# A weight rounding that reads 32-bit tanh values and rounds by adding a constant, instead of a 16-bit integer copy

## The chip, the core and the metric

The kernel runs on one core of one Trainium2 chip. The core has TensorE (matrix products, written to PSUM), VectorE and GpSimd (elementwise work and reductions), ScalarE (activation functions) and SyncE, whose queue issues the DMAs. Each engine works through its own instructions in the order in which they are written; semaphores make one engine wait for another. The metric is device time in microseconds (us), the median of several executions.

## What is computed

For each of 8 batches of 512 rows of width 512, a masked cross-attention over 64 context rows is added to x. Then a gated feed-forward layer with quantized activations and ternary weights (hidden width 2048) is added. The change concerns the ternary weights:

```
def _ternary_quant(w):
    s = jnp.mean(jnp.abs(w))
    wq = jnp.round(jnp.tanh(w / (s + EPS))) * jnp.arctanh(s)
    return w + jax.lax.stop_gradient(wq - w)

def _linear_bit(x, w, g):
    xq = _act_quant(_rmsnorm(x, g))
    wq = _ternary_quant(w)
    return jnp.einsum('bsd,od->bso', xq, wq)

swish = jax.nn.silu(_linear_bit(x, w1, g1))
x_v = _linear_bit(x, w2, g2)
h = swish * x_v
return _linear_bit(h, w3, g3)
```

round(tanh(...)) is -1, 0 or 1; the factor arctanh(s) is applied later, to the result of the product.

## The kernel before

**Tiles.** The 4096 rows are 32 tiles of 128 rows (`NT`), four to a batch (`TPB`). The hidden width is cut into four chunks of 512 (`CH`); the gate works chunk by chunk, `gate(t, 0)` to `gate(t, 3)`.

**Start-up, about the first 95 us.** Each of the three weights comes as 32-bit numbers in four pieces (`WC = 4`, `WN = 2048` elements in each of 128 partitions): the first into `stageA` (the half of `X` that later batches will use), the second into `stageB` (later the space of `hp`, `gh` and `c3`), the third into `stageA` again, piece by piece, once the first weight's piece has been rounded (`load_w3` waits for `s_w1_q`). For each weight: absolute sums of the pieces (`weight_abs`, part on ScalarE, part on VectorE), a matmul with ones that adds over the partitions (`weight_total`), mean and reciprocal on VectorE (`weight_mean`), then for each piece a tanh on ScalarE (`weight_tanh`, L676) and a rounding on VectorE (`weight_round`, L917), which leaves a 16-bit float piece of `W1q`, `W2q` or `W3q`. There are twelve tanh and twelve roundings. Meanwhile GpSimd computes arctanh of the mean as a series of one-column steps, each waiting for the one before (`arctanh_series`, L521 to L527), and from it `wc`; `asc = aa * wc` (L466) is the scale of the silu.

**Between them** stands the first attention and the first tiles: `stage_a_gain` (L826, row times gain, VectorE), `stage_a_root` (avk and ak, L454 and L459, GpSimd), `quantize_12` (L478, GpSimd), a DMA transpose into `q12T`, `up` (L1080, TensorE, which waits for the rounded chunk: `s_w1_q`, `s_w2_q`), `silu` (L655, ScalarE), `gate` (L857, VectorE, silu times second product, into `hp`), `gain_3` (L489, GpSimd, `hp` times the third gain), `max_3` (L863, VectorE), `stage_h_factor`, `quantize_3` (L647, ScalarE), two DMA transposes, `down` (L1092, 16 matmuls, TensorE), `result` (L894, VectorE).

**The loop.** `slot(b, j)` of each engine is one tile's share of that engine's work, in an order written out by hand; it overlaps tile t's up-projection with the down-projection of tile t - 2. The roundings stand at fixed places of VectorE's order: the first weight's 0 at 30 us, 1 at 36, 2 and 3 at 44 directly behind the second's 0; the second's 1 at 48, 2 at 54, 3 at 59; the third's 0 at 82, 1 at 86, 2 and 3 at 88 to 90.

Of the kernel before, what the change touches and what calls it, by code (L numbers as in the profile page):

```python
# [15 lines left out]
ALU = mybir.AluOpType  # L16
ACT = mybir.ActivationFunctionType
# [2 lines left out]
BF16 = mybir.dt.bfloat16  # L20
U8 = mybir.dt.uint8
F16 = mybir.dt.float16
I16 = mybir.dt.int16

P = 128
NEG = 1e30
# [5 lines left out]
MAGIC = 1.5 * 2.0 ** 23  # L32
# [4 lines left out]
def bit_ffn_xattn(nc, x, xT, ctx_rows, mask, maskT, w1T, w2T, w3T, g1, g2, g3, out):  # L37
# [13 lines left out]
    WN = D * H // P // WC  # L51
# [3 lines left out]
    with ExitStack() as ctx:  # L55
        def sb(name, shape, dt=F32):
            return ctx.enter_context(nc.sbuf_tensor(name, shape, dt))
# [53 lines left out]
        winv = sb("winv", [P, 3])  # L111
# [154 lines left out]
        W1f = W1q[:, :, :, :].rearrange("p c k n -> p (c k n)")  # L266
        W2f = W2q[:, :, :, :].rearrange("p c k n -> p (c k n)")
        W3f = W3q[:, :, :].rearrange("p k n -> p (k n)")
# [320 lines left out]
        def _(act):  # L589
# [82 lines left out]
            def weight_tanh(i, src, k, done):  # L672

                act.wait_ge(s_w_inv, i + 1)
                part = slice(k * WN, (k + 1) * WN)
                nc.scalar.activation((W1f, W2f, W3f)[i][:, part].bitcast(I16), src[:, part], ACT.Tanh,  # L676
                                     scale=winv[:, i:i + 1]).then_inc(done, 1)

            def logs(c0, c1, n):
                act.wait_ge(s_coef_arg, 2 * c1)  # L680
# [7 lines left out]
            weight_abs(0, stageA, 2, s_w1_abs)  # L688
            attention_probT(0)
            weight_tanh(0, stageA, 0, s_w1_tanh)  # L690
            weight_tanh(0, stageA, 1, s_w1_tanh)
            stage_a_var(0)
            weight_tanh(0, stageA, 2, s_w1_tanh)
            weight_tanh(0, stageA, 3, s_w1_tanh)
            for k in range(2, WC):
# [61 lines left out]
        def _(dve):  # L757
# [155 lines left out]
            def weight_round(src, dst, k, done_tanh, done):  # L913

                dve.wait_ge(done_tanh, k + 1)
                part = slice(k * WN, (k + 1) * WN)
                nc.vector.tensor_copy(dst[:, part], dst[:, part].bitcast(I16)).then_inc(done, 1)  # L917


            nc.vector.memset(ones[:, :], 1.0).then_inc(s_const_ones, 1)  # L920
# [15 lines left out]
            weight_abs(1, stageB[:, :], 0, s_w2_abs)  # L936
            attention_x1(0, 0)
            weight_round(stageA, W1f, 0, s_w1_tanh, s_w1_q)
            weight_abs(1, stageB[:, :], 1, s_w2_abs)
            dve.wait_ge(s_gains_in, 32)  # L940
            stage_a_gain(0)
            stage_a_max(0)
            stage_a_factor(0, 0)
            weight_round(stageA, W1f, 1, s_w1_tanh, s_w1_q)
            weight_mean(1)
            attention_x1(0, 1)
            attention_cc(1)
            weight_round(stageB[:, :], W2f, 0, s_w2_tanh, s_w2_q)
            weight_round(stageA, W1f, 2, s_w1_tanh, s_w1_q)
            weight_round(stageA, W1f, 3, s_w1_tanh, s_w1_q)  # L950
# [220 lines left out]
```

## Time and profile before

| | us |
|---|---|
| three runs | 476.87, 477.88, 479.64 |
| median | 477.88 |
| the profiled execution | 479.64 |
| its span, first to last instruction | 477.4 |

| engine | busy in the profiled execution |
|---|---|
| TensorE (PE) | 413.4 us, 87% |
| VectorE (DVE) | 400.3 us, 84% |
| ScalarE (ACT) | 351.0 us, 74% |
| GpSimd (POOL) | 331.5 us, 69% |

The profile takes one execution, here the slowest of the three; 2.24 us of it lie outside the span. Engines overlap, so the busy times don't add up to anything; what ends late in each stretch has to be read from the waits. In a row of the timeline the first number is the start in us from the span's start, the second the time from the first start to the last end, then engine, line of the kernel, operation, output and inputs, shapes, and how many instructions are merged in the row; in brackets, how long the engine sat idle before it and what ended that.

### The profile page before, as it was taken

How to read it: one execution, taken by the hardware profiler on the slowest of the kernel's cores; microseconds unless marked ns; L12 is line 12 of the kernel's file. 1: busy time of each engine (PE TensorE's matmuls, PEld its weight loads, DVE VectorE, ACT ScalarE, POOL GpSimd, SP SyncE). 2: the span in 40 equal slices, each digit the busy share in tenths (PEclk: the TensorE clock that was granted, in tenths of full speed). 3: DMA queues.
4: the chain of work that ended last, by engine and by line, in shares of the span. 5: the costliest groups of instructions: out<-in, count | busy, mean ns of one | idle time of the engine just before them, and what ended most of it. 6: DMA issues, size and time to landing. Idle time of an engine off the chain costs nothing. (4 is left out here: it accounts for less than half of the span.)

```text
span 477.4 us, 8317 instructions
## 1 busy us (share of the span) xinstructions
PE 413.4 (87%) x1910; PEld 195.3 (41%) x1910; DVE 400.3 (84%) x913; ACT 351.0 (74%) x608; POOL 331.5 (69%) x535
## 2 busy tenths in 40 slices
PE   0634876899999999999999999999999999899964
PEld 0611622345533464446444644464446434334421
DVE  2496785899999989999999999999999999887550
ACT  1678779987888789867987698869886976565560
POOL 0146647897877777778777877877877878767530
PEclk9999676999999999999999999999999999899988
DMA  6998742354775466645664457455745344435334
GB/s 262 385 384 280 268 176 38 116 110 111 171 174 89 110 181 133 136 110 114 166 170 90 112 144 182 86 119 147 181 86 120 77 88 89 90 78 97 68 70 85
DMA packets 112615, 67.96 MB, mean 142 GB/s; under 512 B 102864, under 2 KB 102992, under 8 KB 108880
## 3 DMA queue, kind: packets, MB, share of 16 engines
q1 hardware_dynamic: 112592, 67.72, 55.1%
q8 instruction: 7, 0.11, 0.1%
q14 instruction: 16, 0.13, 0.1%
HBM read 34.14 MB, written 8.39 MB: 89 GB/s over the span
## 5 line engine op out<-in xcount | busy, mean ns | idle before, releaser
L489 POOL TENSOR_TENSOR stageB<-stageB,g3b 128x512 f32<-128x512 f32 x128 | 164.6, 1290 | 55.0 <-DVE stageB L857 54.2
L1080 PE MATMUL S<-W2q,q12T 128*128 128x512 f16 x512 | 135.7, 389 | 7.4 <-DVE stageB L857 6.1
L1080 PE MATMUL S<-W1q,q12T 128*128 128x512 f16 x512 | 136.0, 389 | 3.8 <-ACT sg L655 2.4
L1092 PE MATMUL DN<-W3q,stageB 128*128 128x512 f16 x512 | 121.3, 391 | 15.4 <-DMA stageB<-stageB 13.7
L655 ACT ACTIVATE sg<-S,asc 128x512 f32<-128x512 f32 x128 | 87.7, 686 | 59.0 <-PE S L1080 53.0
L857 DVE TENSOR_TENSOR stageB<-sg,S 128x512 f32<-128x512 f32 x128 | 86.9, 679 | 16.8 <-ACT sg L655 10.1
L863 DVE TENSOR_REDUCE hm<-stageB 128x1 f32<-128x512 f32 x128 | 86.5, 677 | 1.5 <-POOL stageB L489 1.5
L1092 PEld LDWEIGHTS DN<-W3q,stageB 128*128 128x128 f16 x512 | 49.9, 100 | 81.4 <-issue 26.0
L1080 PEld LDWEIGHTS S<-W2q,q12T 128*128 128x128 f16 x512 | 49.7, 99 | 74.5 <-DVE stageB L857 14.0
L1080 PEld LDWEIGHTS S<-W1q,q12T 128*128 128x128 f16 x512 | 49.6, 100 | 70.6 <-issue 10.0
L662 ACT ACTIVATE junk<-stageB 128x1024 bf16<-128x1024 f32 x64 | 67.3, 1052 | 6.6 <-DVE stageB L857 6.0
L647 ACT ACTIVATE stageB<-stageB,hf 128x1024 f16<-128x1024 f32 x64 | 69.8, 1141 | 2.4 <-DVE hf L880 2.4
L826 DVE SCALAR_TENSOR_TENSOR ga<-X,anm,g12b 128x512 f32<-128x512 f32 x64 | 56.6, 923 | 4.0 <-POOL c L478 2.3
L478 POOL TENSOR_SCALAR c<-ga,af 128x512 f16<-128x512 f32 x64 | 44.0, 699 | 2.1 <-DVE af L848 2.0
L637 ACT ACTIVATE junk_a<-X,anm 128x512 bf16 (+1 forms) x32 | 23.0, 718 | 25.7 <-POOL anm L448 25.7
L832 DVE TENSOR_REDUCE am<-ga 128x2 f32<-128x1024 f32 x32 | 38.8, 1211 | 0.1
L894 DVE SCALAR_TENSOR_TENSOR X<-DN,hsc,X 128x512 f32 (+1 forms) x32 | 24.0, 751 | 16.8 <-PE DN L1092 11.4
L1040 PE MATMUL R<-ccT,xTs 128*128 128x64 f32 x256 | 36.0, 309 | 2.4 <-ACT ccT L594 2.4
L1040 PEld LDWEIGHTS R<-ccT,xTs 128*128 128x128 f32 x256 | 35.9, 225 | 3.9 <-ACT ccT L594 3.1
L459 POOL TENSOR_TENSOR ak<-avk,mhalf 128x1 f32<-128x1 f32 x32 | 27.7, 865 | 2.7
L817 DVE SCALAR_TENSOR_TENSOR X<-R,rval,X 128x512 f32 (+1 forms) x32 | 22.6, 743 | 0.0
L1059 PE MATMUL R<-ctxr,probT 64*128 64x512 f32 x64 | 20.0, 703 | 2.6 <-DVE X L817 2.6
(96 smaller groups left out, 387.4 us busy)
## 6 DMA issues: line engine op xcount, KB each, us to landing
xTs<-in_xT SPq DMA_DIRECT2D x8, 1024.0 KB, 7.1
X<-in_x SPq DMA_DIRECT2D x8, 1024.0 KB, 6.0
out_x<-X SPq DMA_DIRECT2D x32, 256.0 KB, 3.0
X<-in_w1T SPq DMA_DIRECT2D x4, 1024.0 KB, 12.9
stageB<-in_w2T SPq DMA_DIRECT2D x4, 1024.0 KB, 21.5
X<-in_w3T SPq DMA_DIRECT2D x4, 1024.0 KB, 6.5
ctxr<-in_ctx SPq DMA_DIRECT2D x16, 128.0 KB, 3.0
ctxc<-in_ctx SPq DMA_DIRECT2D x8, 128.0 KB, 4.3
```

The source lines that it names most:

```text
L478: nc.gpsimd.tensor_scalar(c12[:, i * D:(i + 1) * D], ga[:, i, :], af[:, i:i + 1], QUANTUM, ALU.mult, ALU.mult).then_inc(s_c12_made, 1)
L489: nc.gpsimd.tensor_tensor(gh[q][:, part], hp[:, part], g3b[:, part], ALU.mult).then_inc(s_gh_made, 1)
L647: nc.scalar.activation(c3[:, part], gh[q][:, part], ACT.Copy, scale=hf[:, :]).then_inc(s_c3_made, 1)
L655: nc.scalar.activation(sg[n % 2][:, :], S1[n % 2][:, :], ACT.Silu, scale=asc[z][:, 0:1])\
L662: nc.scalar.activation(junk[:, h * HALF:(h + 1) * HALF], hp[:, h * HALF:(h + 1) * HALF], ACT.Square, accum_out=hss[:, h:h + 1]).then_inc(s ...
L826: nc.vector.scalar_tensor_tensor(out=ga[:, i, :], in0=xtile(t), scalar=anm[:, :], in1=g12b[:, i, :], op0=ALU.add, op1=ALU.mult).then_inc(s ...
L832: nc.vector.tensor_reduce(am[:, :], ga[:, :, :], AX_X, ALU.max, apply_absolute_value=True)\
L857: nc.vector.tensor_tensor(hp[:, n * CH:(n + 1) * CH], sg[n % 2][:, :], S2[n % 2][:, :], ALU.mult)\
L863: nc.vector.tensor_reduce(hm[:, n:n + 1], gh[q][:, n * CH:(n + 1) * CH], AX_X, ALU.max, apply_absolute_value=True).then_inc(s_gh_max, 1)
L1040: mm = nc.tensor.matmul(R[1][:, j * M:(j + 1) * M], xTs[:, k, j, :], ccT[:, k, :], start=(k == 0), stop=(k == KD - 1))
L1080: mm = nc.tensor.matmul(bank[n % 2][:, :], q12T[q][:, i * KD + k, :], w[:, n, k, :], start=(k == 0), stop=(k == KD - 1))
L1092: mm = nc.tensor.matmul(DN[:, :], q3T[:, k, :], W3q[:, k, :], start=(k == 0), stop=(k == KH - 1))
```

## The change

Before, the tanh writes its values as 16-bit integers into the space of the 16-bit float weight (the conversion rounds them), and VectorE copies them in place from integer to float: 16 bits in, 16 bits out. After, the tanh writes 32-bit floats in place over the loaded piece, and VectorE reads these, adds and subtracts `MAGIC` = 1.5 x 2^23 in one instruction (which rounds to whole numbers) and writes the 16-bit float weight: 32 bits in, 16 bits out. Semaphores, waits and the order of the instructions on every engine stay the same.

```
             def weight_tanh(i, src, k, done):

                 act.wait_ge(s_w_inv, i + 1)
-                part = slice(k * WN, (k + 1) * WN)
-                nc.scalar.activation((W1f, W2f, W3f)[i][:, part].bitcast(I16), src[:, part], ACT.Tanh,
-                                     scale=winv[:, i:i + 1]).then_inc(done, 1)
+                chunk = src[:, k * WN:(k + 1) * WN]
+                nc.scalar.activation(chunk, chunk, ACT.Tanh, scale=winv[:, i:i + 1]).then_inc(done, 1)
...
             def weight_round(src, dst, k, done_tanh, done):

                 dve.wait_ge(done_tanh, k + 1)
-                part = slice(k * WN, (k + 1) * WN)
-                nc.vector.tensor_copy(dst[:, part], dst[:, part].bitcast(I16)).then_inc(done, 1)
+                nc.vector.tensor_scalar(dst[:, k * WN:(k + 1) * WN], src[:, k * WN:(k + 1) * WN], MAGIC, MAGIC,
+                                        ALU.add, ALU.subtract).then_inc(done, 1)
```

## Rows read from the trace of the kernel before

**Rows 1.** Windows: stretch, length, busy us (instructions) per engine, granted clock, DMA.
```profile
70.00:80.00 10.00, 6.04 (x19) 1.96 (x18) 5.05 (x15) 9.91 (x20) 7.28 (x14) 0.67 0.14 26
...
110.00:430.00 320.00, 309.79 (x1511) 146.89 (x1509) 300.03 (x694) 248.81 (x464) 252.40 (x384) 0.99 0.55 125
```

**Rows 2.** Line L917, the roundings: durations in ns (min/median/max), starts, form.
```profile
L917 DVE CAST W1q<-W1q x4: 678/682/686, 30.2 to 45.2; 128x2048 f16<-128x2048 int16 x4
```

**Rows 3.** Timeline of VectorE, 8 to 25 us.
```profile
8.77 0.41 DVE L923 TENSOR_SCALAR mbias<-mask 128x512 f32<-128x512 uint8 x1
...
22.72 2.28 DVE L899 TENSOR_REDUCE wabs<-X 128x1 f32<-128x2048 f32 x1
```

**Rows 4.** Line L524, 40 to 52 us: GpSimd's steps of the series, durations in ns.
```profile
L524 POOL TENSOR_SCALAR ser<-ser,sqr x7: 265/267/3501, 41.7 to 43.8; 128x1 f32<-128x1 f32 x7
```

**Rows 5.** Timeline of all engines, 43.4 to 50 us.
```profile
43.48 3.86 POOL L524 TENSOR_SCALAR ser<-ser,sqr 128x1 f32<-128x1 f32 x2
...
44.00 0.68 DVE L917 CAST W2q<-W2q 128x2048 f16<-128x2048 int16 x1
44.60 1.28 DVE L917 CAST W1q<-W1q 128x2048 f16<-128x2048 int16 x2
...
45.80 1.40 DVE L826 SCALAR_TENSOR_TENSOR ga<-X,anm,g12b 128x512 f32<-128x512 f32 x2
...
47.24 1.22 DVE L832 TENSOR_REDUCE am<-ga 128x2 f32<-128x1024 f32 x1
...
48.37 0.68 DVE L917 CAST W2q<-W2q 128x2048 f16<-128x2048 int16 x1
48.57 0.54 POOL L454 TENSOR_SCALAR avk<-avs 128x1 f32<-128x1 f32 x1 [0.19 <-POOL high L527]
```

**Rows 6.** Timeline of GpSimd, 30 to 90 us.
```profile
30.29 0.61 POOL L527 TENSOR_SCALAR high<-low 128x1 f32<-128x1 f32 x1
...
89.74 1.78 POOL L489 TENSOR_TENSOR stageB<-stageB,g3b 128x512 f32<-128x512 f32 x1
```

**Rows 7.** Timeline of ScalarE, 26 to 98 us.
```profile
26.32 3.89 ACT L676 ACTIVATE W1q<-X,winv 128x2048 int16<-128x2048 f32 x2 [1.84 <-DVE winv L911]
31.30 0.72 ACT L637 ACTIVATE junk_a<-X,anm 128x512 bf16<-128x512 f32 x1 [1.09 <-POOL anm L448]
...
51.06 0.69 ACT L655 ACTIVATE sg<-S,asc 128x512 f32<-128x512 f32 x1 [2.63 <-POOL asc L466]
...
95.60 2.17 ACT L647 ACTIVATE stageB<-stageB,hf 128x1024 f16<-128x1024 f32 x2
```

**Rows 8.** Timeline of VectorE, 59 to 92 us.
```profile
59.14 0.68 DVE L917 CAST W2q<-W2q 128x2048 f16<-128x2048 int16 x1
...
62.40 0.69 DVE L857 TENSOR_TENSOR stageB<-sg,S 128x512 f32<-128x512 f32 x1 [0.86 <-PE S L1080]
...
79.50 0.69 DVE L857 TENSOR_TENSOR stageB<-sg,S 128x512 f32<-128x512 f32 x1 [2.83 <-ACT sg L655]
...
88.63 0.70 DVE L917 CAST W3q<-W3q 128x2048 f16<-128x2048 int16 x1
89.71 0.69 DVE L917 CAST W3q<-W3q 128x2048 f16<-128x2048 int16 x1 [0.37 <-ACT W3q L676]
...
91.56 0.69 DVE L863 TENSOR_REDUCE hm<-stageB 128x1 f32<-128x512 f32 x1 [0.54 <-POOL stageB L489]
```

**Rows 9.** Timeline of TensorE: start-up and end.
```profile
52.06 6.82 PE L1040 MATMUL R<-ccT,xTs 128*128 128x64 f32 x32 [1.91 <-ACT ccT L594]
...
98.49 1.02 PE L1080 MATMUL S<-W1q,q12T 128*128 128x512 f16 x4 [0.65 <-ACT sg L655]
...
447.19 3.61 PE L1092 MATMUL DN<-W3q,stageB 128*128 128x512 f16 x16 [1.08 <-DMA stageB<-stageB]
...
468.36 5.30 PE L1092 MATMUL DN<-W3q,stageB 128*128 128x512 f16 x16 [4.40 <-DMA stageB<-stageB]
```

**Rows 10.** Windows, columns as in rows 1; the granted clock stands behind the five engines.
```profile
60.00:62.00 2.00, 2.00 (x6) 0.71 (x5) 1.54 (x2) 0.69 (x1) 1.27 (x1) 0.50 1.02 430
```

More of the change, by code:

```diff
@@ L22 @@
 F16 = mybir.dt.float16
-I16 = mybir.dt.int16
 P = 128
```

## The prediction

> **What bounds the kernel now.** I read three views, in this order. First the windows: after the start-up the loop keeps TensorE busy for 309.79 of 320 us, so lost time there comes back nowhere; in the start-up, from 70 to 80 us, TensorE is busy for 6.04 us of 10 and ScalarE for 9.91 [rows 1]. The twelve rounding instructions that the change touches all stand in the start-up, between 30 and 90 us. So the question is not what the twelve cost VectorE, but how much later the start-up hands over to the loop. Second, the timeline of the start-up, engine by engine, for who waits for whom. Third, the single rows of VectorE, for the price of the new instruction. In the loop nothing is changed: if all engines enter it later by the same amount, the end is later by that amount.
>
> **The tanh half of the change: nothing.** It writes 32-bit numbers in place instead of 16-bit integers. Two tanh take 3.89 us, about 1.95 apiece in a row. A 512-wide ScalarE activation that writes 32 bits takes 0.69 us (from PSUM), one that writes 16 bits takes 0.72 (from SBUF) [rows 7]: the output's width does not show. The bounds are 0 and a few hundredths of a microsecond each; I take 0. The order of all instructions on all engines and every wait stay as they are, and a load of the third weight into the same space already waits for the rounding, not for the tanh, so no DMA gets a new wait.
>
> **The price of one new rounding.** Now it reads 16 bits and writes 16 bits: 0.68 us for 2048 elements a partition [rows 2]. The new one reads 32 bits and writes 16. Nothing like it stands in the trace, so I bound it. A reduction costs 0.69 us for 512 elements [rows 8] and 2.28 for 2048 [rows 3]: 1.59 / 1536 = 1.04 ns an element, with 0.16 fixed. The same kind of instruction as the new one (two constants, one input, 32 bits out, but 8-bit input) takes 0.41 us for 512 [rows 3]: (0.41 - 0.16) / 512 = 0.49 ns an element, about half of the reduction's. For 2048 this gives 0.16 + 1.00 = 1.16; at exactly half, 0.52, it gives 1.22. I take 1.21, so **+0.53 us** for each rounding. The bounds are +0 (it stays at 0.68) and +1.60 (it runs like the reduction). The page "VectorE: DVE Perf Modes" of the Trainium skill (section on the perf-mode tier table) gives 1227 ns for a 32-bit tensor_scalar of 2048 elements in SBUF; by that the addition would be 0.55, and no row here shows it.
>
> **What hangs on the roundings.** All twelve together are 6.4 us of VectorE, but only those on the path count. Five places.
>
> Step 1, at 30 us. The first rounding starts at 30.16. GpSimd's small step at 30.29 takes 0.61 us and ends with the rounding [rows 6], and ScalarE waits 1.09 us for the step of GpSimd that follows [rows 7]. From there ScalarE has work without a gap until the absolute sums of the second weight, for which the mean and everything at 40 us wait. The longer rounding moves this by **+0.53**.
>
> Step 2, at 44 us, is the main one. GpSimd runs a chain of one-column steps, 0.27 us each; one of them takes 3.50 us [rows 4]. In the timeline the pair that holds it runs from 43.48 to 47.34, while VectorE does one rounding, two more, and the two gain instructions at 45.80; it is free when the reduction at 47.24 begins [rows 5]. So a back-to-back row of such VectorE instructions holds GpSimd up to its end. At the end of GpSimd's chain is the scale asc, for which ScalarE's first silu waits 2.63 us and starts at 51.06 [rows 7]. Three longer roundings: 3 x 0.53 = **+1.59**. What the row shows, a rule explains: the page "SBUF — State Buffer" of the Trainium skill (on the shared port pair) says that VectorE in a two-port mode, or with two SBUF inputs, holds the ports that it shares with GpSimd for the whole instruction. The trace agrees, with 3.50 us in place of 0.27.
>
> Step 3, at 48.4 us. The next rounding does the same to avk: 0.54 us, ending at 49.11, just behind the rounding's 49.05 [rows 5]. Both would start 2.12 later, the rounding ends 0.53 later still: **+0.53**. The first silu is now at 51.06 + 2.65 = 53.7, and TensorE's scores (52.06), which wait for a copy queued behind that silu on ScalarE, are as late. The products of the first tile, from 41 to 50 us, move by about 1 us, since GpSimd's first quantization is held up by a rounding too, but TensorE has them done before it waits 1.91 us ahead of the scores [rows 9]: that wait hides them.
>
> Step 4, 54 to 79 us. Two roundings (one at 59.14, directly ahead of a gate) put VectorE's queue at 2.65 + 1.06 = 3.7. Before the gate at 62.40 VectorE waited 0.86 us for TensorE [rows 8]; that cover is used up and 3.7 - 0.86 = 2.85 remain on VectorE. At 79.50 VectorE waits 2.83 us for a silu of ScalarE [rows 8], so the small surplus goes under and ScalarE's 2.65 counts: **+0**.
>
> Step 5, 82 to 92 us: four roundings of the third weight in a VectorE queue that now idles once, 0.37 us before the last, at 89.71 [rows 8]. Two earlier ones add 1.06, so the third starts at 89.69 (relative to the old clock of events), the last follows directly at 89.69 + 0.60 + 0.53 = 90.82 and ends at 92.03, where it ended at 90.40: +1.63. The gate of tile 2 and the second half of the first down-projection wait for that. GpSimd has it worse: its gain instruction at 89.74 took 1.78 us [rows 6], held up by that last rounding. It ended at 91.52, 1.12 behind the rounding. In a row of roundings without a gap the one-column step ahead of it is shut out too: 92.03 + 0.27 for that step + 1.12 = 93.42, so +1.90. VectorE's reduction at 91.56 waits for that gain (0.54 us of idle) [rows 8], and through it the quantization on ScalarE at 95.60 [rows 7], behind which the silu stands for which TensorE waits 0.65 at 98.49 [rows 9]. So **+1.9**, not less than 1.6.
>
> Sum: 0.53 + 1.59 + 0.53 + 0 + 1.90 = 4.55, rounded up, since the small surpluses of steps 4 and 5 go one way: **+4.6 us**. The profiled execution took 479.64 us, 477.4 of it the span; it would be 482.0 of span and 484.2 in all. That execution is the slowest of the three, so I add to the median: 477.88 + 4.6 = 482.5 us, 1.0% slower.
>
> **Rivals.**
> A: the new rounding costs VectorE 0.53 but GpSimd's stalls don't grow, or shrink. Steps 1 to 3 then cost nothing (the silu waits for GpSimd alone), step 5 about 1.6: +1.6, 479.5 us. For it: no row has this very instruction beside GpSimd. Against it: the old rounding and the new one have one SBUF input each, and the price I take is one at twice the reduction's pace.
> B: it runs like the reduction, +1.60 each. Reductions leave GpSimd alone (it runs again at once under the one at 47.24 [rows 5]), so the queue of VectorE is the path. Up to the gate at 62.40 that is: three roundings and one more before the first gate, +6.4 less about 1.8 of idle that it had before 51.8; two more and 0.86 of cover: at least +3.7 on ScalarE's side by the third weight's mean; then 4 x 1.60 less idle, +5.3. Sum about 9.0, 486.9 us. Against it: the 0.41 us row. By the page "VectorE: DVE Perf Modes" an instruction in the one-element mode would be this case.
> C, the other side, **not slower**: TensorE's clock gives the cost back. It is granted at 0.50 at 60 us, in the middle of the start-up [rows 10], and near the end: a down-projection of 16 matmuls takes 3.61 us at 447.19 and 5.30 at 468.36 [rows 9]; three such blocks are slow (the others at 410.68 and 458.79). Each stands behind a wait for a transpose, and a shifted schedule could meet another grant. All three at full clock give 5.1 back: 482.5 - 5.1 = 477.4. It decides from two of the three on (479.1, no longer slower). Against it: the waits ahead of them move with the shift, so the same lull comes before the same block. In the start-up a faster TensorE gives 0.6 at most, since VectorE's queue (2.85 late) is next.
> D: nothing changes, 477.9: the rounding keeps its 0.68 us.
>
> **Chances.** Forecast (481.2 to 484) 0.66; part of it, by A or by one slow block less (479.3 to 481) 0.14; C in full 0.05; D 0.04; B 0.08; more than forecast otherwise 0.03. The range is 479.3 to 485.6: it leaves out C, D and B. A measurement of this kernel tells about 0.5% (2.4 us) from no change, so "slower" means above 480.3: 0.82; within 0.15 (C, D and half of the partial cases); faster 0.03, if the clock gives back more than all.
>
> **What would show it.** Roundings at 1.2 us each; GpSimd's longest one-column step at 5.1 us, not 3.5; the first silu near 53.7; the wait of 2.83 us at 79.50 still about that; the last rounding of the third weight directly behind the one before, with no idle; the silu and TensorE's wait of 98.49 near 103; from there to the end the same length as before, 379 us. I am wrong if the roundings take 0.7 or 2.3 us, if GpSimd's step does not grow, or if the stretch behind 98 us is shorter or longer by over 1 us.

## The result, and the profile after

| | before | changed |
|---|---|---|
| median of 4 runs each, us | 477.38 | 483.84 |
| lowest to highest | 476.83 to 479.64 | 480.87 to 485.55 |
| profiled execution, us | 479.64 | 481.35 |
| its span | 477.4 | 479.6 |

The ratio is 1.0116, with a 95% interval from 1.0079 to 1.0154: 1.2% slower, against 482.5 us (1.0%) forecast. The ratios here and below are estimates of their own, with an interval, and not the quotients of the medians; here the ratio stands for 5.5 us, while the medians are 6.5 apart. Twenty further executions of the changed kernel, the profiled one among them, are on record; the median of all 24 is 483.44 us. A second set of six runs of the changed kernel (below) gave 1.0125 (1.0093 to 1.0157). The two profiled executions differ by only 2.2 us in span, so they don't tell the whole of it; that difference is taken apart below. One execution of a later kernel (delay, 482.39 us) was over 1.5% above the fastest of its kernel and is left out of its ratio.

The lines that answer to [rows 2] and [rows 4], of the changed kernel: the roundings of the first weight, and GpSimd's steps of the series (durations in ns, min/median/max).

```profile
L914 DVE TENSOR_SCALAR W1q<-X x4: 1214/1217/1251, 29.5 to 46.5; 128x2048 f16<-128x2048 f32 x4
```

```profile
L523 POOL TENSOR_SCALAR ser<-ser,sqr x7: 267/267/5096, 41.9 to 44.1; 128x1 f32<-128x1 f32 x7
```

A rounding takes 1.217 us (forecast 1.21). GpSimd's longest step takes 5.10 us where it took 3.50 (forecast 5.1). And the tanh is as it was: two in 3.90 us. Here is the place itself, the timeline of the changed kernel from 43.7 us on, the answer to [rows 5].

```profile
43.74 5.46 POOL L523 TENSOR_SCALAR ser<-ser,sqr 128x1 f32<-128x1 f32 x2
...
44.25 1.21 DVE L914 TENSOR_SCALAR W2q<-stageB 128x2048 f16<-128x2048 f32 x1
...
45.39 2.35 DVE L914 TENSOR_SCALAR W1q<-X 128x2048 f16<-128x2048 f32 x2
...
47.66 1.40 DVE L824 SCALAR_TENSOR_TENSOR ga<-X,anm,g12b 128x512 f32<-128x512 f32 x2
49.09 1.22 DVE L830 TENSOR_REDUCE am<-ga 128x2 f32<-128x1024 f32 x1
49.28 0.24 POOL L524 TENSOR_SCALAR low<-ws 128x1 f32<-128x1 f32 x1
...
50.23 1.22 DVE L914 TENSOR_SCALAR W2q<-stageB 128x2048 f16<-128x2048 f32 x1
50.43 1.06 POOL L453 TENSOR_SCALAR avk<-avs 128x1 f32<-128x1 f32 x1 [0.19 <-POOL high L526]
```

The picture is that of before, only stretched: GpSimd is held from the first rounding to the reduction, and the next rounding catches avk (1.06 us, 0.54 before). ScalarE then waits, the answers to [rows 7]:

```profile
31.55 0.72 ACT L636 ACTIVATE junk_a<-X,anm 128x512 bf16<-128x512 f32 x1 [1.72 <-POOL anm L447]
...
53.45 0.69 ACT L654 ACTIVATE sg<-S,asc 128x512 f32<-128x512 f32 x1 [4.76 <-POOL asc L465]
...
99.94 2.18 ACT L646 ACTIVATE stageB<-stageB,hf 128x1024 f16<-128x1024 f32 x2
```

VectorE and TensorE, the answers to [rows 8] and [rows 9]:

```profile
65.03 0.69 DVE L855 TENSOR_TENSOR stageB<-sg,S 128x512 f32<-128x512 f32 x1
...
81.90 0.69 DVE L855 TENSOR_TENSOR stageB<-sg,S 128x512 f32<-128x512 f32 x1 [2.60 <-ACT sg L654]
...
92.09 2.38 DVE L914 TENSOR_SCALAR W3q<-X 128x2048 f16<-128x2048 f32 x2
...
95.90 0.69 DVE L861 TENSOR_REDUCE hm<-stageB 128x1 f32<-128x512 f32 x1 [0.67 <-POOL stageB L488]
```

```profile
54.45 7.09 PE L1038 MATMUL R<-ccT,xTs 128*128 128x64 f32 x32 [1.06 <-ACT ccT L593]
...
102.83 1.02 PE L1078 MATMUL S<-W1q,q12T 128*128 128x512 f16 x4 [0.88 <-ACT sg L654]
```

```profile
414.71 3.61 PE DN L1090 x16
...
470.52 5.31 PE DN L1090 x16
```

(The last fence is from the chain of waits.) The gate that waited 0.86 us for TensorE now waits for nothing; the 2.83 at 79.50 is 2.60 at 81.90; the last two roundings of the third weight follow each other without a gap; TensorE's wait has moved from 98.49 to 102.83, by 4.34 (by 4.73 against the reciprocal that serves as zero below, which comes 0.39 us earlier here). Step 5's other sign is there as well, the one-column step shut out under the last roundings (0.19 us before):

```profile
93.47 1.04 POOL L535 TENSOR_SCALAR wc<-ser 128x1 f32<-128x1 f32 x1
```

From TensorE's wait to the end it is 376.8 us, against 378.9 before, because one of the three down-projections at TensorE's slow pace (the one that stood at 410.68, 5.30 us) now takes 3.61. That is not shown to be the change's doing: of the 14 profiled executions of this document ten have two slow down-projections, w3_new and f16_magic among them, and four have three (before, delay, after_moved, before_warm).

**A ruler for the start-up.** Executions begin a few tenths of a microsecond apart, and the early rows move with that. So I measure from VectorE's first reciprocal near 22 us (rinv), which stands ahead of all that is changed, to four later points of one profiled execution each: ScalarE's first silu, its second logarithm (of the third weight's series), and its first and second quantization pair (q3 of tiles 0 and 1); then the end of the span.

| kernel | first silu | logarithm | q3, tile 0 | q3, tile 1 | end |
|---|---|---|---|---|---|
| before | 28.69 | 49.54 | 57.83 | 73.23 | 455.0 |
| changed | 31.47 | 52.34 | 60.63 | 77.96 | 457.6 |
| changed, again | 31.27 | 52.92 | 61.21 | 78.54 | 459.0 |
| three_new | 30.40 | 51.52 | 59.80 | 75.20 | 456.7 |
| w12_new | 31.25 | 51.55 | 59.84 | 75.25 | 455.7 |
| w3_new | 28.71 | 49.46 | 57.74 | 75.04 | 454.4 |
| delay | 28.72 | 47.91 | 56.20 | 73.08 | 455.1 |
| f16_magic | 28.61 | 47.80 | 56.08 | 71.75 | 452.1 |
| three_acc | 26.19 | 52.70 | 60.98 | 76.38 | 454.9 |
| before_moved | 27.61 | 45.83 | 54.11 | 69.51 | 450.0 |
| after_moved | 29.14 | 49.99 | 58.27 | 76.31 | 458.6 |
| before_warm | 28.57 | 47.66 | 55.94 | 72.40 | 455.1 |
| after_warm | 31.16 | 51.31 | 59.59 | 77.50 | 459.0 |
| moved_warm | 27.33 | 45.53 | 53.81 | 69.20 | 449.8 |

### The profile page after: what moved, and what is told of

Read it like the earlier page. It is cut to its first block and busy times, and to the rows that moved or that the text cites. A ratio compares the mean times of both kernels' runs of the same rounds, so it can differ in the third digit from the quotient of the medians.

```text
span 479.6 us, 8317 instructions
## 1 busy us (share of the span) xinstructions
PE 412.8 (86%) x1910; PEld 195.2 (41%) x1910; DVE 406.7 (85%) x913; ACT 351.0 (73%) x608; POOL 337.5 (70%) x535
## 5 line engine op out<-in xcount | busy, mean ns | idle before, releaser
L1090 PE MATMUL DN<-W3q,stageB 128*128 128x512 f16 x512 | 119.7, 387 | 16.1 <-DMA stageB<-stageB 12.8
```

Of the source, the lines that this page charges most:

```text
L1090: mm = nc.tensor.matmul(DN[:, :], q3T[:, k, :], W3q[:, k, :], start=(k == 0), stop=(k == KH - 1))
```

## The experiments

### One place at a time: three_new, w12_new, w3_new

In these the old and the new form stand side by side, chosen for each piece by a list:

```
+                to = src[:, part] if (i, k) in NEW else (W1f, W2f, W3f)[i][:, part].bitcast(I16)
+                nc.scalar.activation(to, src[:, part], ACT.Tanh, scale=winv[:, i:i + 1]).then_inc(done, 1)
...
+                if (i, k) in NEW:
+                    nc.vector.tensor_scalar(dst[:, part], src[:, part], MAGIC, MAGIC, ALU.add, ALU.subtract).then_inc(done, 1)
+                else:
+                    nc.vector.tensor_copy(dst[:, part], dst[:, part].bitcast(I16)).then_inc(done, 1)
```

three_new: only the three of the row at 44 us.

> Only the three roundings of the row at 44 us (second weight 0, first weight 2 and 3) read 32-bit values; the other nine stay 16-bit copies. My theory (each longer rounding in a back-to-back row holds GpSimd up by its whole extra): GpSimd's longest step 3.50 + 1.6 = 5.1 us, first silu 1.6 later than 51.06, and the end 1.4 to 1.7 us later (median near 479.0). Rival (the cost is VectorE's queue, GpSimd does not matter): GpSimd's step stays at 3.5, the first silu moves by under 0.3 us, the end by at most 0.5.

478.99 us against 477.95, ratio 1.0034 (1.0013 to 1.0056), 1.6 us by the ratio. GpSimd and ScalarE:

```profile
L525 POOL TENSOR_SCALAR ser<-ser,sqr x7: 264/265/5098, 41.6 to 43.7; 128x1 f32<-128x1 f32 x7
```

```profile
52.53 0.69 ACT L656 ACTIVATE sg<-S,asc 128x512 f32<-128x512 f32 x1 [4.21 <-POOL asc L467]
```

The longest step is 5.10 us, the first silu 1.71 later on the ruler (1.59 forecast). Step 2 is right.

w12_new: the eight of the first two weights.

> The eight roundings of the first two weights read 32-bit values, the four of the third stay 16-bit copies. My theory (steps 1 to 4): first silu 2.65 later, wait of VectorE at 79.5 still 2.6 to 2.8, end +2.65 us (median near 480.0). Rival (the extra of the changed kernel beyond 4.6 us arises here): +4 or more.

481.93 us against 477.95, ratio 1.0094 (1.0064 to 1.0124): 4.5 us by the ratio, from four executions. The silu is 2.56 later on the ruler, as steps 1 to 3 say (2.65). But 2.65 us would be 0.55%, outside the interval. Something behind the silu is missing from the sum. The profiled execution, the fastest of the four, doesn't show it: its logarithm is 2.0 later than before, its end 0.7.

w3_new: the four of the third weight.

> Only the four roundings of the third weight read 32-bit values. My theory (step 5): nothing moves before 82 us; the silu of ScalarE and TensorE's wait at 98.49 are 1.9 later, the end too (median near 479.3). Rival (the down-projection alone waits for them, and the loop takes it in): TensorE's wait at 98.49 later by under 1 us and the end by under 1 us.

478.21 us against 477.95, ratio 1.0031 (0.9997 to 1.0065). Nothing moves up to q3 of tile 0 (57.74, 57.83 before), and from there to q3 of tile 1 it is 17.30 us where it was 15.40: +1.90, what step 5 says, and the changed kernel has 17.33. The time (1.5 us by the ratio) agrees, though its interval just reaches zero. The rival, that the loop takes it in, has q3 at under 1 us later and is out. Both together give 0.94 + 0.31 = 1.25%; the changed kernel has 1.16 and 1.25%. Each of the two parts is known to about 0.3% only.

### Is it the hold on GpSimd, or VectorE's time? three_acc

The same three instructions, but in the form that also writes out a sum. They multiply by one and add zero, so this kernel leaves out the rounding of these three pieces. The cut is shown against three_new:

```
-                    nc.vector.tensor_scalar(dst[:, part], src[:, part], MAGIC, MAGIC, ALU.add, ALU.subtract).then_inc(done, 1)
+                    nc.vector.tensor_scalar(dst[:, part], src[:, part], 1.0, 0.0, ALU.mult, ALU.add, accum_out=racc[:, 4 * i + k:4 * i + k + 1]).then_inc(done, 1)
```

> As three_new, but the three instructions at 44 us multiply by one and add zero and also write out a sum (the rounding of these three pieces is left out, so their weights are unrounded tanh values). If this form runs at the reduction's pace and leaves GpSimd alone: 2.2 to 2.3 us each, 4.8 more of VectorE's time than before, yet GpSimd's longest step falls to 0.3 us and the first silu comes at 48.3 to 49.5 although VectorE is busy longer; the first gate waits for VectorE. That would show that the wait of three_new was for what the roundings hold and not for VectorE. Rival (GpSimd waits for VectorE in some other way, by its time): GpSimd's step grows to 8 us and the silu comes near 56.

The timeline of all engines, around 44 us:

```profile
42.92 1.08 POOL L526 TENSOR_SCALAR ser<-ser,sqr 128x1 f32<-128x1 f32 x3
...
43.79 2.27 DVE L921 TENSOR_SCALAR_CACHE_REDUCE W2q<-stageB 128x2048 f16<-128x2048 f32 x1
44.09 0.24 POOL L527 TENSOR_SCALAR low<-ws 128x1 f32<-128x1 f32 x1
...
48.34 0.69 ACT L657 ACTIVATE sg<-S,asc 128x512 f32<-128x512 f32 x1
...
54.39 0.68 DVE L859 TENSOR_TENSOR stageB<-sg,S 128x512 f32<-128x512 f32 x1
```

VectorE is busy nearly twice as long as with the new rounding (2.27 us each), and GpSimd runs through under it at 0.27 us a step; the first silu comes 4.2 us earlier than in three_new. So GpSimd waits for what the rounding holds, not for VectorE's time. The page "SBUF — State Buffer" of the Trainium skill (section "Who interferes with whom") excepts this form from the operations that can take the ports; the run agrees. It is no remedy: now VectorE's own queue is late (the first gate at 54.39), and the time is 479.84 us, ratio 1.0054 (1.0032 to 1.0076).

### The width or the operation? f16_magic

The tanh writes 16-bit floats, and VectorE does the same add and subtract on them in place:

```
-                nc.vector.tensor_copy(dst[:, part], dst[:, part].bitcast(I16)).then_inc(done, 1)
+                nc.vector.tensor_scalar(dst[:, part], dst[:, part], MAGIC, MAGIC, ALU.add, ALU.subtract).then_inc(done, 1)
```

(The tanh values are rounded to 16 bits before they are rounded to whole numbers, which moves those next to one half.)

> All twelve: the tanh writes 16-bit floats into the weight's space, and VectorE adds and subtracts the same constant there, 16 bits in and 16 bits out. It tells the operation from the width. Theory: the width alone sets the price, so 0.68 us each, GpSimd's step stays near 3.5 and the time within 1 us of the kernel before. Rival: adding and subtracting costs, 1.2 us each, and the time is as the changed kernel's (+4.6 or more).

```profile
L917 DVE TENSOR_SCALAR W1q<-W1q x4: 675/680/691, 29.8 to 44.9; 128x2048 f16<-128x2048 f16 x4
```

0.680 us, as the copy, and 478.34 us against 478.29, ratio 1.0002 (0.9982 to 1.0023). Adding and subtracting cost nothing over the copy; the 32-bit input is the whole price.

### A better place: before_moved, after_moved

```
-            weight_round(stageA, W1f, 2, s_w1_tanh, s_w1_q)
-            weight_round(stageA, W1f, 3, s_w1_tanh, s_w1_q)
             stage_a_gain(1)
...
                 else:
+                    weight_round(stageA, W1f, 2, s_w1_tanh, s_w1_q)
+                    weight_round(stageA, W1f, 3, s_w1_tanh, s_w1_q)
                     weight_round(stageB[:, :], W2f, 2, s_w2_tanh, s_w2_q)
```

> The kernel before, with the first weight's roundings 2 and 3 moved in VectorE's order from 44.6 us to behind the first gate (52.5), where VectorE idles 1.5 us. Theory: GpSimd's held-up step shrinks by 1.2 us (3.5 to 2.3), the first silu comes at 49.0 to 49.9 instead of 51.06, and the end 1.2 to 2.2 us earlier (median near 475.8). Rival (GpSimd is not what sets the silu): first silu unmoved, end within 0.3.

474.47 us against 478.29, ratio 0.9933 (0.9909 to 0.9958), 3.2 us by the ratio: faster than both kernels. GpSimd's longest step is 2.30 us and the silu 1.08 earlier on the ruler; the expectation fell short, since up to the logarithm it is 3.7. Part of the rest comes from TensorE. Its scores (for before, see [rows 9]):

```profile
51.17 3.79 PE L1040 MATMUL R<-ccT,xTs 128*128 128x64 f32 x32
```

They take 3.79 us where they took 6.82. They stand directly behind the products of the first tile, while before TensorE had idled 1.91 us ahead of them. From the silu to the logarithm it is 18.22 us here, 20.85 before, and 19.09 in before_warm (below), where the scores are as fast but nothing is moved. So about 1.8 us of the 3.7 go with TensorE's pace and 0.9 with VectorE's shorter queue (ScalarE's wait for arg, which comes out of that queue, is 0.49 us here and 1.29 in before_warm).

> The changed kernel with the same move. Theory: GpSimd's held-up step shrinks from 5.1 by 2.3 us, the first silu comes 2.3 us earlier than 53.45, and the end about 2 us earlier than the changed kernel's, 2.4 to 3 later than before. Rival: as above, no gain.

481.63 us, ratio 1.0072 (1.0044 to 1.0100), so 0.5% less than the changed kernel beside it; the silu is 2.13 to 2.33 earlier. The longest step is 2.84 us, 2.26 less. The scores took 6.91 us in this execution.

### Does a late start pass through the loop? delay

```
+                if first and j == 2:
+                    dve.wait_ge(s_gain3_in, 16)
+                    for e in range(2):
+                        nc.vector.tensor_reduce(hdelay[:, e:e + 1], g3b[:, :], AX_X, ALU.add)
                 gate(t, 0)
```

> The kernel before with two plain reductions of 2048 elements (2 x 2.28 us, which do not hold GpSimd) put into VectorE's order ahead of the first gate of tile 2, near 90 us: a delay at the handover to the loop without any change of the roundings. My theory (the loop passes a late start on one to one): 3.6 to 4.5 us later at 98.49 and the same amount at the end. Rival (the changed kernel's median is 6 us later, over the 4.6 of the steps, because a late loop meets a lower granted clock): the end moves by 1.5 to 2 us more than the wait at 98.49, at a lower mean clock in most runs. Second rival (the loop recovers): the end moves by under 3 us.

A miss: 477.34 us (median of all ten) against 477.95, ratio 0.9982 (0.9950 to 1.0013), no difference. The two reductions took 4.47 us of VectorE, but from q3 of tile 0 to q3 of tile 1 only 1.48 appear (16.88 against 15.40): GpSimd and ScalarE had gone on, so VectorE's waits for them fell away. The delay was no delay of the handover, so this run doesn't answer its question. What it does show is that VectorE time alone at this place, directly behind the last rounding, is two thirds hidden. The four roundings of the third weight are 2.1 us of VectorE for a loss of 1.9. That they cost so much because they hold GpSimd as well fits the changed kernel's trace (the GpSimd step of 1.04 us at 93.47, and VectorE's wait of 0.67 us for GpSimd's gain at 95.90), but no run parts the two for this weight. The 1.48 us don't appear in the runs; they went from 474.5 to 482.4 us, a wide spread.

### Where the rest comes from: after_again, before_warm, after_warm, moved_warm

> The changed kernel once more beside the kernel before. Theory of the steps: +4.6 us. Open is why its median was 6.5 above. If the excess is the granted clock, runs at the same mean clock as the kernel before's differ by 4 to 5 us and the rest spreads by 4 us with the clock; if the steps are sized too small, all runs lie over 5.5 above.

483.75 us against 478.29, ratio 1.0125 (1.0093 to 1.0157), 6.0 us. The runs lie at 481.2 to 486.4, those of the kernel before beside it at 476.4 to 481.3. The spread is the same on both sides, and the medians are 5.5 apart. Neither alternative of the expectation fits as it stands. Of the changed kernel's 30 executions, the first set and this one, eight have a mean granted clock of 0.980 or more and took 480.87 to 481.64 us; the other 22, at 0.956 to 0.974, took 482.95 to 486.38. None of the 77 executions of the kernel before that were run beside the experiments is above 0.975. The profiled execution with its 2.2 us is one of the eight. What the two groups do differently is open: this kernel's profiled execution (0.959) has the same two slow down-projections, and ends 1.35 us later on the ruler, 0.58 of it at q3 of tile 0.

The forecast's step 4 let a wait for TensorE (0.86 us at 62.40) hide the two roundings there. That wait depends on TensorE's pace. In the four executions with 16-bit roundings in the first two weights and nothing moved, the logarithm came at 49.54, 49.46, 47.91 and 47.80 on the ruler; the scores took 6.82, 7.09, 6.16 and 6.07 us. The first execution, on which the forecast rests, was one of the two slow ones. In three with 32-bit roundings the logarithm came at 52.34, 52.92 and 51.55. The means are 48.68 and 52.27: +3.6, not +2.65. To make the pace equal, three kernels got idle matmuls where TensorE waits:

```
+            def keep_busy(n):
+                for _ in range(n):
+                    nc.tensor.matmul(DN[:, P:2 * P], ones[:, :], identf[:, :], start=True, stop=True)
...
+            pe.wait_ge(s_w_totred, 1)
+            keep_busy(20)
             weight_total(1, s_w2_abs)
+            pe.wait_ge(s_w_totred, 2)
+            keep_busy(4)
...
+                if first and j == 0:
+                    keep_busy(5)
```

(and `keep_busy(3)` ahead of the first W2 product).

> The kernel before, with 32 idle matmuls (ones by identity, into an unused part of a bank, read by nobody) put into TensorE's order where it only waits: 20 from 32 us, 4 at 40, 3 at 43, 5 ahead of the scores at 52. The scores should take 3.8 us instead of 6.8, the stretch from the first silu to the first quantization of a tile about 26.5 us instead of 29.1, and the end should be 2 to 3 us earlier than before. If the pace of TensorE does not set that stretch: within 0.5 us of before.

> The changed kernel with the same 32 idle matmuls. Both at TensorE's full pace, VectorE's queue is what is late behind the first silu, so the two roundings of step 4 are no longer hidden by its wait for TensorE: 2.65 + 1.06 + 1.9 = 5.6 us over the same kernel with 16-bit roundings. Rival (the excess over 4.6 in the changed kernel's median comes from TensorE's slow pace alone): with the pace made equal only 4.6 remain, or less.

TensorE's scores in before_warm and in after_warm:

```profile
52.98 3.68 PE L1040 MATMUL R<-ccT,xTs 128*128 128x64 f32 x32
```

```profile
54.96 4.32 PE L1038 MATMUL R<-ccT,xTs 128*128 128x64 f32 x32
```

Near the full pace in both, the logarithm comes at 47.66 and 51.31: **+3.65**, which is 2.59 at the silu and 1.06 from there to the logarithm (20.15 against 19.09), the two roundings of step 4 uncovered. ScalarE now waits there for VectorE's and GpSimd's queue, the same 1.29 us in both kernels (after_warm shown):

```profile
73.23 0.21 ACT L679 ACTIVATE lns<-arg 128x2 f32<-128x2 f32 x1 [1.29 <-POOL arg L515]
```

The times are 478.54 and 483.44 us, ratios 1.0012 (0.9987 to 1.0036) and 1.0138 (1.0097 to 1.0180): 1.3% or 6.0 us apart. The 5.6 expected (1.17%) agrees with that, but the rival's 4.6 (0.96%) isn't excluded by it, since the two intervals together leave about 0.5% either way. What speaks against the rival is the traces' 3.65 up to the logarithm. The two profiled executions don't carry the 5.6 to the end: they are 5.1 apart at q3 of tile 1, since both meet TensorE's slow pace on the way (16.46 and 17.91 us from q3 to q3), and 3.9 at the end, where before_warm has three slow down-projections and after_warm two. The idle matmuls themselves gained nothing, against the expectation: before_warm is 1.9 us ahead at q3 of tile 0, but in that execution TensorE was at its slow pace from 88 to 94 us (eight matmuls of the first down-projection in 3.57 us, 2.01 before), q3 of tile 1 is only 0.8 ahead, and the end is not ahead at all.

> The kernel before with the first weight's roundings 2 and 3 moved behind the first gate, and the idle matmuls. If the gain of the move (3.8 us) was 1.1 from the silu and the rest from TensorE's pace, this ends at the pace of the moved kernel, 474 to 475 us, and 1 us ahead of the kernel with idle matmuls alone. If both gains add in full: 471 to 472.

474.15 us, ratio 0.9943 (0.9914 to 0.9972), at the pace of before_moved; the gains don't add.

## Why the prediction was right, point by point

**Price of one rounding: right.** 1.217 us measured, 1.21 taken. The bounds of 0.68 and 2.28 were not needed; f16_magic shows that the input's width decides.

**The tanh: right,** 3.90 us for two, 3.89 before.

**Step 1: right in its mechanism.** ScalarE's wait at the changed kernel's 31.55 is 1.72 us, 1.09 before: +0.63 for a forecast 0.53. The rounding now starts earlier against GpSimd's chain and catches another of its steps (1.38 us, 0.34 before).

**Steps 2 and 3: right.** On the ruler the silu comes 2.78 and 2.58 later in the two executions of the changed kernel, 2.65 forecast; 1.71 of it from three_new's row. three_acc and the moved kernels show that it is the hold on GpSimd.

**Step 4: mis-sized, the one real error.** It was put at 0, and is 1.06 us when TensorE is at its full pace in that stretch (warm pair) and nothing in the profiled execution at the slow pace (from the silu to the logarithm 20.87 us, 20.85 before; the second execution of the changed kernel has 21.65). I took the cover from one execution without asking what would take it away. With 1.0 for it the sum is 5.6 us or 1.17%, against 1.16% and 1.25% measured; with 0 it is 0.96%, inside both intervals too, but w12_new's interval (from 0.64%) leaves out the 0.55% that steps 1 to 4 would then give.

**Step 5: right.** 17.33 us from q3 of tile 0 to q3 of tile 1, in w3_new 17.30, 15.40 before: +1.9. The step ahead of GpSimd's gain was shut out as forecast (1.04 us, ending at 94.51, just behind the last rounding's 94.47).

**One to one to the end: not shown apart.** The traces fit it (from q3 of tile 1 to the end 378.5 to 382.7 us in all kernels, with no trend by how late it is), but this spread is as large as the cost. delay against f16_magic fits as well: with the logarithm at the same place it is 1.3 later at q3 of tile 1 and 3.0 at the end, where it has one slow down-projection more. In the profiled execution rival C came true by a third: one slow down-projection of three was at full pace, which gave 1.7 of the 4.3 back. Since other kernels have that too, this was the luck of the execution rather than the shift, as far as is shown; the medians, 6 us apart, show nothing given back.

**Rivals.** A falls with GpSimd's 5.10 us step, B with the 1.217 us, D with both. The forecast of 379 us behind 98.49 was 376.8 in the trace, outside the 1 us that I had allowed; the down-projection at full pace explains 1.7 of it. By that sign of being wrong the forecast failed here. The execution itself took 481.35 us, 2.9 less than the 484.2 forecast for it, and the median 1.3 more than forecast: the two misses go opposite ways. With 1.0 for step 4 the forecast of the median would have been 483.5, 0.3 below what was measured. The chances given for "slower" add up to 0.84, not 0.82.

What stays open: how often TensorE is at which pace in the start-up. The runs without a profile show a mean clock only, so the step from 4.6 to 5.6 us rests on seven traces and one pair of kernels.

## What to carry to other kernels

Before making a VectorE instruction longer or shorter, look at which GpSimd steps start under it: here 0.5 us more on an instruction delayed a chain of 0.27 us steps by as much each time, and moving two of the 16-bit roundings out of the row gained 0.7%, twice what the three longer ones in the row cost (0.3%) and over half of what the whole change costs. Keep 16-bit input where the values allow it, and put instructions that hold GpSimd where GpSimd has nothing to do that someone waits for. A cover read in one execution (0.86 us of waiting for TensorE) is worth as much as the pace that TensorE has in the others.

## What the runs showed of the hardware that was not expected

- VectorE instructions that hold GpSimd, in a row without a gap, hold it to the end of the row: 5.10 us across three roundings and two gains. The forecast relied on it, from one row of 3.50 us; the runs show it at every length tried (2.30, 2.84, 3.50, 5.10 us), for GpSimd steps of one column that alone take 0.27 us.
- The form of the instruction with a sum as second output runs at 2.27 us for 2048 elements, 1.9 times as long, and leaves GpSimd alone.
- The granted clock column (behind the five engines) reads 1.00 in the changed kernel's window from 56 to 62 us, while the scores, from 54.45 on, take 7.09 us, almost twice the 3.79 of before_moved. The kernel before reads 1.00 from 40 to 50 us as well, while four matmuls of an up-projection take 1.89 us there (1.03 later). So a 1.00 in the start-up doesn't show the full pace; the durations of the matmuls do.

```profile
56.00:62.00 6.00, 6.00 (x28) 5.64 (x29) 5.67 (x4) 5.36 (x7) 3.48 (x4) 1.00 0.82 227
```

- Thirty-two idle matmuls brought the scores to 3.68 us, and the time did not fall: in that execution the slow pace came at 88 us instead, and in after_warm's at 92.
